# Attention stage: q, k and V units in a PSUM bank of their own, spread over the steps; denominators in 32-column tiles; rotation by token halves

## The reference

```
x = x + attention(layernorm(x), Wq, bq, Wk, bk, Wv, bv, Wo, bo)
x = x + ffn(layernorm(x), w_gate, w_up, w_down)

attention: q, k, v = x @ W + b, split in 16 heads; q, k = apply_rope(q), apply_rope(k)
    scores = einsum("bnqd,bnkd->bnqk", q, k) / sqrt(64); causal mask
    attended = softmax(scores) @ v;  return attended @ Wo + bo
ffn: h = silu(fp4_linear(x, w_gate)) * fp4_linear(x, w_up);  return fp4_linear(h, w_down)
fp4_linear(x, w) = fp4_quant_dequant(x) @ fp4_quant_dequant(w).T
```

## Time and profile before

| | us |
|---|---|
| median of 3 runs (1281.27 to 1288.55) | 1287.2 |
| profiled execution, its own time | 1286.15 |
| its span on core 4, the slowest | 1284.1 |
| spans of the eight cores | 1262.5 to 1284.1 |
| stage 2 on core 4 | 97.8 to 612 |

### The profile page before, as it was taken

The page is one execution under the profiler, slowest core; times in us unless marked ns, Lnnn a source line. Parts: engine busy times, 40 slices in busy tenths (PEclk is TensorE's granted clock), DMA queues, the critical chain, the costliest instruction groups (busy, mean ns, idle before and its releaser), DMA issues.

```text
span 1283.9 us, 18262 instructions; the slowest of 8 cores (1262.5 to 1284.1 us)
## 1 busy us (share of the span) xinstructions
PE 1095.1 (85%) x6112; PEld 462.1 (36%) x6112; DVE 1041.7 (81%) x1199; ACT 763.6 (59%) x1000; POOL 104.1 (8%) x203
## 2 busy tenths in 40 slices
PE   1898988989798888867986889899998999999996
PEld 0342232323232223222332444444444444444443
DVE  4597997788788999989845788888888888888885
ACT  3577788788788888988545434344444434334432
POOL 1011011111111110122100000000000000000000
PEclk9899999999999999988998889899898989899998
DMA  9955787677777775799997100000000000000000
GB/s 214 255 120 144 142 164 152 112 176 129 170 161 163 154 145 121 176 227 218 217 255 228 46 33 17 17 34 33 33 34 34 33 33 25 26 17 34 17 18 33
DMA packets 108923, 139.94 MB, mean 109 GB/s; under 512 B 76256, under 2 KB 79776, under 8 KB 107936
## 3 DMA queue, kind: packets, MB, share of 16 engines
q1 hardware_dynamic: 91792, 90.27, 29.1%
q0 software_dynamic: 15312, 42.22, 16.0%
q10 hardware_dynamic: 1728, 6.29, 1.5%
HBM read 96.29 MB, written 27.13 MB: 96 GB/s over the span
## 4 chain that ended last, share of the span: by engine, by line
PE 42%; DVE 22%; DMA 12%; issue 11%; ACT 9%; POOL 1%; DVEq 1%; SPq 0%; ACTq 0%; POOLq 0%
PE ps L1311 16%; PE ps L683 6%; PE ps L971 5%; PE ps L1355 5%; ACT PT L953 4%; PE ps L927 4%; DVE sm_bm L300 3%; PE ps L654 3%; DMA rb<-rscr 2%; DMA rscr<-rn 2%; PE ps L1278 2%; DMA qx<-wd 2%; DVE h_u L1342 2%; DVE h_u L314 2%; DVE h_y L332 2%
## 5 line engine op out<-in xcount | busy, mean ns | idle before, releaser
L953 ACT ACTIVATE PT<-ps,nb 128x1024 bf16<-128x1024 f32 (+1 forms) x320 | 301.1, 995 | 12.1 <-PE ps L927 5.8
L319 ACT ACTIVATE h_y<-h_u 128x1024 f32<-128x1024 f32 (+1 forms) x48 | 47.3, 986 | 288.3 <-DVE h_u L314 288.3
L1311 PE MATMUL ps<-wgT,xqT 128*128 128x512 bf16 (+1 forms) x768 | 192.6, 399 | 6.0 <-ACT h_u L1333 4.4
L1311 PE MATMUL ps<-wuT,xqT 128*128 128x512 bf16 (+1 forms) x768 | 173.4, 370 | 0.0
L1355 PE MATMUL ps<-wdT,hqT 128*128 128x512 bf16 x704 | 162.6, 384 | 5.6 <-ACT hqT L1284 5.6
L927 PE MATMUL ps<-qk 64*128 64x512 bf16 (+3 forms) x640 | 116.9, 357 | 47.2 <-ACT PT L953 30.8
L683 PE MATMUL ps<-xlT,wqk 128*128 128x512 bf16 x512 | 124.2, 386 | 25.5 <-ACT PT L953 24.4
L971 PE MATMUL ps<-PT,vat 128*64 128x512 bf16 (+3 forms) x640 | 121.6, 376 | 0.4
L971 PE MATMUL ps<-PT,ones 128*64 128x512 bf16 (+3 forms) x640 | 114.1, 354 | 0.0
L1311 PEld LDWEIGHTS ps<-wgT,xqT 128*128 128x128 bf16 x768 | 79.5, 106 | 90.9 <-issue 33.2
L1311 PEld LDWEIGHTS ps<-wuT,xqT 128*128 128x128 bf16 x768 | 77.1, 100 | 84.2 <-issue 13.0
(11 more groups left out here) (94 smaller groups left out, 1496.6 us busy)
## 6 DMA issues: line engine op xcount, KB each, us to landing
qx<-wu SPq DMA_DIRECT2D x22, 512.0 KB, 5.4
qx<-wg SPq DMA_DIRECT2D x22, 512.0 KB, 5.7
x_a<-x SPq DMA_DIRECT2D x16, 512.0 KB, 16.9
qx<-wd SPq DMA_DIRECT2D x16, 512.0 KB, 5.1
x_t<-x POOLq DMA_DIRECT2D x16, 512.0 KB, 8.4
out<-x_t SPq DMA_DIRECT2D x16, 512.0 KB, 2.6
sw<-qk POOLq DMA_DIRECT2D x56, 128.0 KB, 4.4
rb<-rscr POOLq DMA_DIRECT2D x28, 256.0 KB, 5.9
```

Of the source, the lines that this page charges most:

```text
L319: return act((lambda c: c.activation(y[:, 0:F], u[:, 0:F], AFT.Abs, scale=2.0 ** 22)), [(sDVE, v4)] + list(y_free))
L953: exp_a[n] = act((lambda c: c.activation(PT[j].ap()[:, :, o:512], sc[:, :, o:512], AFT.Exp, bias=nb12.ap(), scale=0.125)), ws, cost=0.31 + ...
L1311: ins = te.matmul(bank[:, 0:cn], xqT[t % 2].ap()[:, kc, :], w.ap()[:, n0:n1, kc, :], start=(kc == 0), stop=(kc == KC - 1))
```

## The change

- q, k and V work is written as units (`qk_unit`, `v_unit`). In attention they no longer take score tiles: all go, one after the other, to one bank of their own, `F_BANK`, the second half of `PS[3]`, and `fill_to` issues after each step's `av` as many matmuls as keep pace with the 40 steps (2.5 a step in pairs 0 to 3, 1.6 in pairs 4 to 6), never past the end of a unit in one call. A unit's first matmul waits for the eviction of the unit before. In stage 1 `unit_now` issues a whole unit in a ring tile, as before.
- O of both parities shares `PS[2]` (one bank each), and denominators of both parities share the first bank of `PS[3]`: the ones matrix has 32 columns, and block parity and head pick the 32 partitions (`den_row`). `od_evict` copies 64 partitions of denominators, and `norm_gather` of a whole pair takes eight DMAs instead of two.
- Units are ordered by token block: q, k (and V) of block 0, then of block 1, and so on. `swap` and `rope` work on q and k together for a half of the tokens (1024). Scores of a pair wait for the first half at step 0 and for the second at step 12, where query block 2 begins. Both rotations of pair p + 1 used to be done in pair p; now the second falls into pair p + 1.
- In the last pair the weight chunks of the gate matrix may go straight to their place in SBUF from step 12 on, not from step 2.
- Output projection 0 to 3 waits for all copies out of PSUM.

```diff
-    ones64 = misc("ones64", [128, 64], BF16, 128)
+    ones32 = misc("ones32", [128, 32], BF16, 64)
...
-        def qk_half(p, which, tb):
...
+        def qk_unit(p, which, tb):
+            def mm(te, o, i):
+                return te.matmul(
+                    o, wqk[p % 2].ap()[:, i, which * 128:which * 128 + 128],
+                    xlT.ap()[:, i, tb * 512:(tb + 1) * 512],
+                    start=(i == 0), stop=(i == KC - 1))
+
+            def evict(o, pp):
+                a = qk_a[p, which, tb] = act((lambda c: c.activation(
                     raw[p % 2].ap()[:, which, tb * 512:(tb + 1) * 512],
-                    PS[k].ap()[:, 0:512], AFT.Identity,
+                    o, AFT.Identity,
                     bias=bqk.ap()[:, 2 * p + which:2 * p + which + 1],
                     scale=1.0)),
                     [(sPE, pp), (sBQ, bqk_ld)]
                     + ([(sPE, s_last[p - 2])] if p >= 2 else []), cost=0.7)
                 if p == 0 and which == 1:
                     swap_first(tb)
-                elif p and tb == 3:
-                    swap(p, which)
-            slot_task[k] = ("qk", p, which, tb)
-            act_later(("qk", p, which, tb), [(sPE, pp)], evict)
-
-        def swap(p, which):
-            w = [(sACT, qk_a[p, which])]
-            if p >= 1:
-                w.append((sDVE, rope_tb[3] if p == 1 else
-                          rope_v[p - 1, which]))
+                elif p and which == 1 and tb % 2 == 1:
+                    swap(p, tb // 2)
+                return a
+            w = [(sWQ[p % 2], wq_ld[p]), (sACT, a_evac[4 * tb + 3])]
+            return ("qk", p, which, tb), KC, mm, evict, w
...
+        def unit_now(u):
+            name, n, mm, evict, w = u
+            k = ring()
+            o = PS[k].ap()[:, 0:512]
...
+        fill = {"units": [], "i": 0, "free": 0, "task": None, "done": 0}
+        def fill_to(count):
+            while fill["units"] and fill["done"] < count:
+                name, n, mm, evict, w = fill["units"][0]
+                i0 = fill["i"]
+                if i0 == 0:
+                    if fill["task"] is not None:
+                        act_need(fill["task"])
+                        fill["task"] = None
+                    w = w + [(sACT, fill["free"])]
+                else:
+                    w = []
+                i1 = min(n, i0 + count - fill["done"])
+                fill["done"] += i1 - i0
+                def f(te, i0=i0, i1=i1, mm=mm):
+                    ins = None
+                    for i in range(i0, i1):
+                        ins = mm(te, F_BANK, i)
+                    return ins
+                pp = pe(f, w, cost=0.235 * (i1 - i0))
+                fill["i"] = i1
+                if i1 < n:
+                    continue
+                if name[0] == "qk":
+                    qk_p[name[1]] = pp
+                fill["units"].pop(0)
+                fill["i"] = 0
+                def run(evict=evict, pp=pp):
+                    fill["free"] = evict(F_BANK, pp)
+                fill["task"] = name
+                act_later(name, [(sPE, pp)], run)
+                return
...
+        def swap(p, h):
+            w = [(sACT, max(qk_a[p, n, 2 * h + j] for n in range(2)
+                            for j in range(2)))]
+            w.append((sDVE, rope_tb[2 * h + 1] if p == 1 else
+                      rope_v[p - 1, h]))
+            sl = slice(1024 * h, 1024 * h + 1024)
             for g in range(4):
                 o, i = 32 * g, 32 * (g ^ 1)
-                sw_d[p, which] = dma(
-                    "gpsimd", sSW[which], sw.ap()[o:o + 32, which, :],
-                    raw[p % 2].ap()[i:i + 32, which, :], w, lag=8.0)
-            dve_later(("rope", p, which),
-                      lambda: [(sSW[which], sw_d[p, which]), (sTAB, tab)],
-                      lambda: rope(p, which))
-
-        def rope(p, which):
-            q = raw[p % 2].ap()[:, which, :]
-            s = sw.ap()[:, which, :]
-            dve((lambda v: v.tensor_tensor(q, q, cosb[:], Alu.mult)),
-                [(sSW[which], sw_d[p, which]), (sTAB, tab)])
-            v2 = dve((lambda v: v.tensor_tensor(s, s, sinb[:], Alu.mult)), [])
-            rope_v[p, which] = dve((lambda v: v.tensor_tensor(
+                sw_d[p, h] = dma(
+                    "gpsimd", sSW[h], sw.ap()[o:o + 32, :, sl],
+                    raw[p % 2].ap()[i:i + 32, :, sl], w, lag=8.0)
+            dve_later(("rope", p, h),
+                      lambda: [(sSW[h], sw_d[p, h]), (sTAB, tab)],
+                      lambda: rope(p, h))
...
+        def den_row(qb, h):
+            return 64 * (qb % 2) + 32 * h
...
+            m = 512 // w
+            for c in range(a, b, 512):
+                for h in range(2):
+                    r = den_row(c // 512, h)
+                    o = 64 * h + (c - a) // w
+                    d = dma("gpsimd", sDN[k], dn[k].ap()[o:o + m, 0:w],
+                            den.ap()[r:r + 1, c:c + 512]
+                            .rearrange("o (p f) -> o p f", f=w), ws)
...
-        HALF = {1: (0, 0), 5: (0, 1), 8: (0, 2), 12: (0, 3),
-                15: (1, 0), 19: (1, 1), 22: (1, 2), 26: (1, 3)}
-        V_AT = {10: 0, 28: 1, 32: 2, 36: 3}
+        F_BANK = PS[3].ap()[:, 512:1024]
...
-            ws = ([(sDVE, rope_tb[qb])] if p == 0 else
-                  [(sDVE, rope_v[p, 0]), (sDVE, rope_v[p, 1])])
+            ws = [(sDVE, rope_tb[qb] if p == 0 else rope_v[p, qb // 2])]
...
-            od = PS[2 + k].ap()
+            od = PS[2].ap()[:, 512 * k:512 * k + 512]
+            dp = PS[3].ap()[:, 0:512]
 
             def f(te):
                 ins = None
-                for dst, w in ((0, None), (512, ones64)):
-                    for h in range(2):
-                        lhs = (vat.ap()[:, p + 1, kc, 64 * h:64 * h + 64]
-                               if w is None else ones64[:])
-                        ins = te.matmul(
-                            od[64 * h:64 * h + 64, dst + o:dst + 512], lhs,
-                            PT[j].ap()[:, h, o:512], start=(kc == 0),
-                            stop=(kc == 4 * qb + 3), skip_group_check=True)
+                for h in range(2):
+                    te.matmul(
+                        od[64 * h:64 * h + 64, o:512],
+                        vat.ap()[:, p + 1, kc, 64 * h:64 * h + 64],
+                        PT[j].ap()[:, h, o:512], start=(kc == 0),
+                        stop=(kc == 4 * qb + 3), skip_group_check=True)
+                for h in range(2):
+                    r = den_row(qb, h)
+                    ins = te.matmul(
+                        dp[r:r + 32, o:512], ones32[:],
+                        PT[j].ap()[:, h, o:512], start=(kc == 0),
+                        stop=(kc == 4 * qb + 3), skip_group_check=True)
...
+            units = []
+            for tb in range(4):
+                if p + 1 < NP:
+                    units += [qk_unit(p + 1, 0, tb), qk_unit(p + 1, 1, tb)]
+                if p < 4:
+                    units.append(v_unit(4 * p + tb, 1))
+            total = sum(u[1] for u in units)
+            fill["units"] = units
+            fill["done"] = 0
...
+                if p and kc == 0 and qb % 2 == 0:
+                    for tb in (qb, qb + 1):
+                        for n in range(2):
+                            act_need(("qk", p, n, tb))
+                    dve_need(("rope", p, qb // 2))
...
-                if p < 4 and s in V_AT:
-                    v_proj(4 * p + V_AT[s], 1)
-                if p + 1 < NP and s in HALF:
-                    which, tb = HALF[s]
-                    qk_half(p + 1, which, tb)
+                fill_to(total * (s + 1) // 40)
...
+            while fill["units"]:
+                fill_to(total)
...
+                start_wo()
+            if s == 12:
                home["g"] = [(sPE, qk_p[NP - 1]), (sPE, s_last[NP - 2]),
...
-                w += [(sACT, sc_free[i])] if i < 2 else [(sACT, od_free[i - 2])]
+                w.append((sACT, max(sc_free + od_free + [fill["free"]])))```

PE in pair 1, query block 1 into block 2, before. L683 is a q or k unit, L927 scores, L934 masks, L971 O and then denominators:

```order
L927 MATMUL ps1<-qk1_81 128x512 x2
L971 MATMUL ps2<-PT3_85,vat_74 64x128 x2
L971 MATMUL ps2<-PT3_85,ones64_45 64x128 x2
L927 MATMUL ps0<-qk1_81 128x512 x2
L971 MATMUL ps3<-PT4_86,vat_74 64x512 x2
L971 MATMUL ps3<-PT4_86,ones64_45 64x512 x2
L683 MATMUL ps1<-xlT_73,wqk0_78 128x512 x8
L927 MATMUL ps0<-qk1_81 128x512 x2
L971 MATMUL ps3<-PT5_87,vat_74 64x512 x2
L971 MATMUL ps3<-PT5_87,ones64_45 64x512 x2
```

105 lines of the change are left out of this document (51 added, 54 removed).

## The result

The changed kernel takes 1318.5 us (median of 4 runs) against 1284.2 for the kernel before, beside it on the same chip; the ratio is **1.0251, 95% interval 1.019 to 1.0313**. The forecast was 1277, the range 1260 to 1300. The profiled execution took 1317.96 us; its slowest core, 1, spans 1316.4.

The account below looks back on a forecast made before the run. PE was taken as the bound in pairs 0 to 3, DVE in pairs 5 and 6. Pairs 1 to 3 -2, pair 0 -3.5, pairs 4 to 6 -4.7, pair 7 +1.3: 1286.15 - 9 = 1277 us, range 1260 to 1300.

Parts of the forecast that it names:

- PE's prices: PE in attention: 0.11 us a change of tile shape; 32-column denominators add 0.08 a step, 3.2 us a pair.
- Rival (a): Denominators on PE: 32-column tiles cost no change of shape; whole 1266 us; chance 0.15.
- (b): Pieces on PE: a seam costs 0.10 us more, from unhidden weight loads; whole 1303 us; chance 0.17.
- The missing 8 us are the lumps: Pairs 1 to 3: PE's time without work, 8 us a pair, comes from units issued whole in score banks; spreading removes it.
- 0.1 us a unit: Unit bank: PE's waits for the eviction of the unit before, 0.1 us a unit, 1.3 a pair.
- Pair 0, -3.5: First pair: a quarter of its 15.5 us beyond PE's work is given back, -3.5 us.
- Pairs 4 to 6, -4.7: DVE holds these pairs near 61 us; 186 us against 190.7, most of the gain in pair 4.
- 0 to 1 us a pair: Denominator gather, eight transfers instead of two: ACT's next copy waits for it, cover about nothing, 0 to 1 us a pair.
- rival (c): Late gather stalls ACT's copy and exps, or rotated half is late at step 12; 2.5 us, seven pairs; 1295 us; chance 0.14.
- Three more tiles through scratch, no engine waiting: Last pair: direct gate weights from step 12, not 2, send three more tiles through scratch on SP, at no cost.
- Pair 7 was forecast at +1.3: Last pair: only diagonal steps are PE's, 16 x 0.08 us, +1.3 us.
- The rotation by halves at zero: Rotation by token halves on DVE: same six operations, no cost; second half ready with 3 us of cover at step 12.

Follow-up runs that it names:

- e1: Kernel before with only the denominators through 32 columns of ones instead of 64; whole 0.36% longer, mean of the cores 1278.4 us against 1269.6.
- e17: e14 with the 2 MB load of wo at step 28 of pair 6; ratio 1.0013 to the kernel before.
- e18: e17 with whole units of eight or nine matmuls in place of pieces of four; over the whole, e17 is faster by 5 us (0.4%).
- e8: e7 with 64 columns of ones again and one bank and one set of partitions for all denominators; ratio 1.0124 to the kernel before.
- e10: e8 with the 2 MB load of wo at step 12 of the last pair instead of step 2; ratio 1.0130 to the kernel before.
- e12: e10 with units in pieces of four matmuls instead of two or three; 0.002 of the whole less than e10.
- e14: e12 with the load of wo back at step 2 and the last rotation ahead of pair 7; ratio 1.0042 to the kernel before.
- e15: e14 with pieces ended at step 26 and the rotation ahead of the next pair in pairs 4 to 6; ratio 1.0082 to the kernel before.
- e2: Changed kernel with two gather transfers a pair instead of eight; pairs 1 and 6 shorter by 2.8 and 4.7 us, pair 5 longer by 3.4.
- e7: Changed kernel with two gathers, denominator partitions by pair parity, pieces ended at step 32, gate tiles' place free at step 2; ratio 1.0216 to the kernel before.
- e4: Kernel before with only the gate tiles' place freed at step 12 of the last pair instead of step 2; ratio 1.0117.
- e13: e7 with pair 6's pieces ended at step 26 and the last rotation ahead of pair 7 in DVE's order; ratio 1.0173 to the kernel before.
- e11: Kernel before with only q and k units in turn and swap and rotation by token halves; no difference, in no pair.
- e3: Changed kernel with each q, k or V unit issued whole instead of in pieces; ratio within 1.010 to 1.020 of the kernel before.

## Why the prediction was wrong, step by step

- **PE's prices were right.** 0.11 us a change of shape, 0.08 more a step for 32 columns: 0.33 after, 0.34 in e1; PE's work grew by 5.9 and 6.6 us in pairs 2 and 4, forecast 6.1 and 6.5. Rival (a) is refuted (0.33, not 0.24), and so is (b): its extra 0.10 a seam is not in the rows (a piece of three 0.76, of two 0.54).
- **"The missing 8 us are the lumps" was the step that failed.** The prediction counted PE's waits for ACT over all pairs (42.3 us in 171 to 560, 7 us a pair) and booked nearly all of it as gone. It took what PE did not do for what the lumps cost. In pair 2, the least disturbed, PE's idle time fell from 7.9 us to 3.5 (medians of the cores), while its work grew by 5.9: the pair is 1.6 us longer. About half of even that fall needs no spreading: in e1 idle falls by 1.9 us in pair 1 (2.2 in pair 2, medians) because PE has more to do. And at equal tile shapes pieces of four leave more idle time than whole units in pair 1 (7.7 us in e17, 6.0 in e18, 5.9 before): they take 2.7 us off PE's wait for exp before scores, not 8, and the waits for the banks take its place. So in pairs 1 to 3 there was nothing to win against the seams.
- **"0.1 us a unit" for the bank** was mis-sized: 22.1 us in 25 waits on core 4, near 4 us a pair. The walk over full steps was right for full steps, but a unit that ends beside a block's end or an abs pass waits up to 2.2 us (5.5 at the most), and the granted clock then falls.
- **Pair 0, -3.5:** the changed kernel ends it at 170.4 us (median) against 169.9 before, no gain. A gain of 6 us was there: with 64 columns it ends at 166.3 and 165.6 (e8, e10), with pieces of four as well at 163.2 to 164.1 (e12, e14, e15, e17), and with whole units at 163.7 (e18). So the 32 columns ate 4 us of it and the short pieces 2; the gain itself does not come from pieces.
- **Pairs 4 to 6, -4.7:** most of it was to come from pair 4, read on core 4, where it took 66.5 us. At the median of the cores it took 60.2 before, so there was little to win; the changed kernel takes 61.2, on core 4 too. DVE's floor near 60 us held (59.0 to 61.9 us in pair 4, except with whole units). What was missing in pairs 5 and 6 is the gather.
- **The gather at "0 to 1 us a pair", with a cover of about nothing.** The cover was read rightly, and rival (c) named the wait, at 0.14. Its price, 2.5 us a pair, is of the size of what the runs gave back in pairs 6 (4.7, e2) and 5 (6.4, e7). Not in pair 1: the 2.8 us of e2 are gone again in e7, whose gather lands in 2.3 us on every core and whose pair 1 takes 71.8. The step that failed is the landing time: 3.2 us, the median of before, was taken for a queue in which the same change moves four swaps right ahead of the gather. The prediction says so itself ("it stands behind the four swaps") and counted only their issue (1.93 us), not that they load the same DMA engines.
- **"Three more tiles through scratch, no engine waiting"** was the costliest line, at zero. e4 has two more tiles: pair 7 grows by 8.9 us and the whole by 1.2% (interval 0.4 to 1.9). e7 and e13 show the rest: also with the old place for the tiles, pair 7 is 8 us longer when the last store leaves just behind wo's load. Pair 7 was forecast at +1.3 and got +11.7.
- **The rotation by halves at zero** was right for itself (e11), and its cover of 3 us at step 12 was enough: no wait of scores for DVE stands there on any core. What it cost was elsewhere: the last swap beside the gather, and the last rotation, which ends 13 to 15 us into pair 7 (before the change it had ended by 0.6 us into it).
- **A slip in rival (a):** 13 us less than 1277 is 1264, not 1266. It changes nothing in the verdict.

Shares of the loss, as far as the runs part them, by the mean of the cores: the changed kernel is at 1304.8 us, the kernel before at 1269.6 to 1271.8 in the experiments, so 33 to 35 us. The 32 columns are 8.8 (e1) or 8.2 (e7 to e8). The gate tiles' place, the late rotation and the gathers together are about 15 (e13 is still 19.2 above before); the gate tiles' place alone costs 12.1 in e4, so the parts don't add. Some 10 us are left. They may be the pieces and the waits for their bank, but no run shows it: e18, without pieces, is no faster than e17. Open as well: why pair 1 still takes 2.3 us more with pieces of four than before at a granted clock of 1.00 (67.6 against 65.3). The intervals of e2, e3 and e7 are too wide to order them.

## What to carry to other kernels

Idle time of an engine is not a price until the rows say what it waited for, and a wait that is counted over a whole stage has to be read pair by pair: work added to a full engine is certain, while the stall that it should remove may have other causes. Of a step that is moved to the end of a stage, look at what else leaves there: a small transfer that an engine waits for should leave ahead of the bulk and not behind it. Here a gather of 8 KB that left 1 us behind four swaps took 12.4 us to land (1.8 at best), and a store that left 0.3 us or more behind a 2 MB load of another queue took 6.8 us or more (3.1 or less ahead of it). And where one in-order engine serves two streams (here exp and the abs pass of the weights), a late transfer in the one stream stops the other; an edit "with no engine waiting" needs the chain read to its end.

## What the runs showed of the hardware

A gather of 8 KB that lands in 1.8 us at its best took 12.4 beside swaps, weights and a copy inside DRAM, with the DMA engines at a share of 1.0 to 1.5 and only 57 to 81 GB/s. A store of 256 KB from SyncE landed in 2.0 to 3.1 us when it left ahead of POOL's 2 MB load or with it, and in 6.8 to 11.8 when it left 0.3 to 3.5 us behind it (before, e7, e8, e13 to e15). A transposing transfer held SyncE's queue for 10.17 us while an earlier transpose, weight loads and loads of x were under way (e7); the same instruction takes 1.24 us later in pair 7 of the kernel before (576.14 us, core 2). And a stall costs twice: after 5 us in which PE did 0.30 us of work the granted clock was 0.50 (1.2 GHz) for the next five. One such fall adds some 1.5 us to a pair (67.6, 69.2 and 70.7 us with none, one and two in e17's pair 1).
